# Two-layer graph kernel: the maxima of gathered neighbours accumulate in a PSUM bank, the third and fourth tile come earlier in the program, and layer 0 and the neighbour codes share one bank

## The reference, cut to what matters

```
h = relu(layernorm(x))                                   # (8, 2048, 256)
idx = the 25 smallest j with adj[n, j] != 0              # per node
agg = max over idx of h[idx]          (>= 0 if there are 25 or fewer)
x = x + relu(concat(h, agg) @ W0 + b0)                   # layer 0
h = relu(layernorm(x));  hidden = h @ W1.T
attn = leaky_relu(hidden @ a[0] + (hidden @ a[1]).T), masked, softmax
x = x + attn @ hidden + bias                             # layer 1
```

## Time and profile before

| what | value |
|---|---|
| median of 3 runs | 4676.5 us (4674.2 to 4679.66) |
| the profiled execution, its own time | 4680.8 us |
| its span, first to last instruction | 4679.0 us |
| GpSimd busy | 3481.4 us (74%) in 3204 instructions |
| VectorE busy | 2768.3 us (59%) |
| TensorE matmul busy | 2578.4 us (55%), mean granted clock 0.714 of full speed |
| ScalarE busy | 1470.9 us (31%) |

### The profile page before, as it was taken

How to read it: one execution, slowest core, us unless ns; L and a number is a source line. 1 busy time by engine, 2 the same in 40 slices (tenths; PEclk the granted TensorE clock), 3 DMA queues, 4 the chain that set the end, 5 groups by cost and what they waited for, 6 DMA issues and landing times.

```text
span 4679.0 us, 39010 instructions
## 1 busy us (share of the span) xinstructions
PE 2578.4 (55%) x10074; PEld 1682.2 (36%) x10074; DVE 2768.3 (59%) x6213; ACT 1470.9 (31%) x1489; POOL 3481.4 (74%) x3204
## 2 busy tenths in 40 slices
PE   1222245565655565655566565565665556565589
PEld 0111133343433343333344333343443334343356
DVE  5444456566666565665665665656666556665655
ACT  3111233323333232333232333332333323333234
POOL 5777777777777777777777777777777777777730
PEclk7555566777766777776677767677776777776789
DMA  7444555545555545555555555554555554544430
GB/s 265 159 149 156 171 174 177 193 160 189 185 178 195 173 165 194 174 180 199 169 182 179 177 177 197 171 193 162 181 182 188 184 182 159 186 169 153 147 109 32
DMA packets 228389, 809.23 MB, mean 173 GB/s; under 512 B 59466, under 2 KB 60372, under 8 KB 207828
## 3 DMA queue, kind: packets, MB, share of 16 engines
q0 software_dynamic: 153600, 419.64, 28.9%
q1 hardware_dynamic: 56308, 321.91, 18.7%
q10 hardware_dynamic: 18432, 67.12, 3.5%
HBM read 690.98 MB, written 119.54 MB: 173 GB/s over the span
## 4 chain that ended last, share of the span: by engine, by line
POOL 74%; issue 21%; PE 3%; DMA 1%; ACT 0%; DVE 0%; POOLq 0%; SPq 0%; DVEq 0%; ACTq 0%
POOL near L461 74%; PE acc L1302 2%; PE pen L1291 0%; PE pen L1288 0%; DMA nmask_dram<-nm_t 0%; DMA adj_i<-in_adj_dram 0%; DMA table_dram<-near 0%; DVE near L836 0%; ACT near L665 0%; PE bank L1273 0%; PE acc L1263 0%; ACT nm_t L506 0%; POOLq L458 0%; PE bank L1241 0%; DMA near<-table_dram,idx 0%
## 5 line engine op out<-in xcount | busy, mean ns | idle before, releaser
L461 POOL DMA_INDIRECT near<-table_dram,idx x3200 | 3481.2, 1088 | 1012.9 <-issue 975.2
L836 DVE TENSOR_TENSOR near<-near 128x3072 f32<-128x3072 f32 (+3 forms) x512 | 866.0, 1691 | 1214.6 <-DMA near<-table_dram,idx 1200.8
L1302 PE MATMUL acc<-hid,wgt 128*128 (+1 forms) x4096 | 1012.0, 405 | 79.2 <-ACT wgt L544 76.2
L1302 PEld LDWEIGHTS acc<-hid,wgt 128*128 128x128 f32 x4096 | 812.9, 203 | 206.4 <-issue 79.7
L1233 PE MATMUL bank<-cst,h_q 128*128 128x128 f32 x256 | 84.5, 431 | 1304.0 <-DVE agg L839 1292.7
L614 ACT ACTIVATE h_t<-bank 128x512 f32<-128x512 f32 x128 | 76.4, 597 | 1739.9 <-PE bank L1235 1739.9
L1241 PE MATMUL bank<-w_sb,h_t 128*128 128x256 f32 x1024 | 476.7, 646 | 98.0 <-ACT h_t L614 98.0
L1233 PEld LDWEIGHTS bank<-cst,h_q 128*128 128x128 f32 x256 | 35.5, 195 | 1346.5 <-DVE agg L839 1102.0
L506 ACT ACTIVATE nm_t<-adj_i,big_c 128x2048 bf16<-128x2048 int32 x128 | 499.8, 3954 | 5.0 <-DMA adj_i<-in_adj_dram 5.0
L924 DVE SCALAR_TENSOR_TENSOR wgt<-pen,a_slope,lin 128x512 f32<-128x512 f32 x512 | 361.1, 746 | 223.3 <-PE pen L1291 172.3
L539 ACT ACTIVATE lin<-a_b,a_rise 128x512 f32<-128x512 f32 x468 | 317.3, 718 | 430.8 <-DVE wgt L924 408.2
(11 more groups left out here) (137 smaller groups left out, 2125.5 us busy)
## 6 DMA issues: line engine op xcount, KB each, us to landing
adj_i<-in_adj_dram SPq DMA_DIRECT2D x128, 1024.0 KB
nmask_dram<-nm_t ACTq DMA_DIRECT2D x128, 512.0 KB, 7.6
nm_q<-nmask_dram SPq DMA_DIRECT2D x29, 2048.0 KB, 8.4
near<-table_dram,idx POOLq DMA_INDIRECT x3200
h_q<-table_dram SPq DMA_DIRECT2D x32, 512.0 KB, 3.9
x_q<-in_x_dram SPq DMA_DIRECT2D x32, 512.0 KB, 5.0
xmid_dram<-x_q SPq DMA_DIRECT2D x32, 512.0 KB
o_q<-xmid_dram SPq DMA_DIRECT2D x32, 512.0 KB, 6.3
```

The lines of the kernel that those rows point to most:

```text
L461: pool.indirect_dma_start(out=near[:, t % 2, k, :], out_offset=None, in_=table, in_offset=bass.IndirectOffsetOnAxis(ap=idx[:, t, k:k + 1], ...
L836: nc.vector.tensor_tensor(rows[:, lo:count, :], rows[:, lo:count, :], rows[:, other:other + count, :], ALU.max).then_inc(mx_step, 1)
L1302: mm = nc.tensor.matmul(acc[:, t, 0:C + 1], wgt[:, c % 2, i * QR + t * P:i * QR + (t + 1) * P], hid[:, bass.ds(batch * NJ + j, 1), 0:C + 1 ...
```

## The change

The maxima no longer fold `near` onto itself. The first `tensor_tensor` of a tile takes two pairs of rows (512 elements each) from `near` and writes `highest`, a PSUM tile of one bank; ten more take the next pair from `near` and `highest` and write `highest` again; then row 25 with the first half of `highest` goes to `agg`, and `agg` with its second half to `agg`. `agg` now has two halves in turn. `highest` takes the place of `bank2`, so the neighbour codes and layer 0's output go through `bank1` as well, and each user of `bank1` on TensorE waits for both semaphores that free it (`bank_free`). In VectorE's order the maxima of tile 2 move into the index rounds of pair 0 (`third_tile`), those of tile 3 ahead of chunk 4; TensorE and ScalarE do `layer0` 2 and 3 and their copies after chunks 1 and 4 in place of 3 and 7; `index_prep` of pair 0 comes after `attend_setup` on TensorE.

```diff
-        agg = sb("agg", [P, C], F32)
+        agg = sb("agg", [P, 2, C], F32)
-        bank2 = psum("bank2", [P, 512], F32)
+        highest = psum("highest", [P, 2 * C], F32)
@@ ScalarE, step @@
-                for c in range(1, 4):
+                for c in range(1, 8):
                     attended(c)
-                gathered()
-                for c in range(4, 8):
-                    attended(c)
-                gathered()
+                    if c in (1, 4):
+                        gathered()
@@ VectorE, index_words and residual0 read bank1 in place of bank2 @@
-                words = bank2[:, :].rearrange("p (u g) -> p u g", u=2)
+                words = bank1[:, :].rearrange("p (u g) -> p u g", u=2)
@@ VectorE, maximum @@
-                rows = near[:, t % 2, :, :]
-                folds = [(0, 12, 13), (0, 6, 7), (0, 3, 4), (0, 2, 2)]
-                for n, (lo, count, other) in enumerate(folds):
-                    nc.vector.tensor_tensor(rows[:, lo:count, :], rows[:, lo:count, :],
-                                            rows[:, other:other + count, :], ALU.max).then_inc(mx_step, 1)
-                    dve.wait_ge(mx_step, n + 1)
-                nc.vector.tensor_tensor(agg[:, :], rows[:, 0, :], rows[:, 1, :], ALU.max).then_inc(agg_made, 1)
+                pair = lambda k: near[:, t % 2, k:k + 2, :].rearrange("p a c -> p (a c)")
+                mx_n = Count()
+                nc.vector.tensor_tensor(highest[:, :], pair(0), pair(2), ALU.max).then_inc(mx_step, 1)
+                for k in range(4, S - 1, 2):
+                    dve.wait_ge(mx_step, mx_n.next())
+                    nc.vector.tensor_tensor(highest[:, :], pair(k), highest[:, :], ALU.max).then_inc(mx_step, 1)
+                dve.wait_ge(mx_step, mx_n.next())
+                nc.vector.tensor_tensor(agg[:, t % 2, :], near[:, t % 2, S - 1, :], highest[:, 0:C], ALU.max
+                                        ).then_inc(mx_step, 1)
+                dve.wait_ge(mx_step, mx_n.next())
+                nc.vector.tensor_tensor(agg[:, t % 2, :], agg[:, t % 2, :], highest[:, C:2 * C], ALU.max).then_inc(agg_made, 1)
@@ VectorE, step @@
-                def after_first():
+                def third_tile():
                     finished(1)
+                    gathered(2)
                     attended(2)
 
+                def fourth_tile():
+                    finished(3)
+                    attended(6)
+
                 if "index" in stages:
-                    index_write(0, woven(after_first, 1, 3))
+                    index_write(0, woven(third_tile, 1, 3))
+                    finished(2)
                     index_words(s + 1, 1)
...
-                gathered(2)
+                gathered(3)
                 attended(4)
-                finished(2)
-                rest = "index" in stages and lo < LAST - 1
-                if rest:
-                    ix_n = woven(lambda: attended(6), 5, 7)
+                if "index" in stages and lo < LAST - 1:
+                    index_write(1, woven(fourth_tile, 5, 7))
                 else:
-                    attended(5, 6, 7)
-                gathered(3)
-                if rest:
-                    index_write(1, ix_n)
+                    attended(5)
+                    fourth_tile()
+                    attended(7)
                 if "attend" in stages:
                     attend_end(a)
-                finished(3)
@@ TensorE @@
+            def bank_free():
+                pe.wait_ge(b1_free, b1.n + 1)
+                pe.wait_ge(b2_free, b2.n + 1)
...
                 gathered(0)
+                if "attend" in stages:
+                    attend_setup(a)
                 if "index" in stages:
                     index_prep(s + 1, 0)
-                if "attend" in stages:
-                    attend_setup(a)
                 gathered(1)
-                for c in range(4):
+                for c in range(8):
                     if "attend" in stages:
                         chunk(a, c)
+                    if c == 1:
+                        gathered(2)
                     if "index" in stages and c == 2:
                         index_prep(s + 1, 1)
-                gathered(2)
-                for c in range(4, 8):
-                    if "attend" in stages:
-                        chunk(a, c)
-                gathered(3)
+                    if c == 4:
+                        gathered(3)
```

More of the change, by code:

```diff
@@ L1254, in project @@
                 pe.wait_ge(h2t_made, q + 1)
-                pe.wait_ge(b1_free, b1.next())
+                bank_free()
+                b1.next()
                 for k in range(KC):
```

29 lines of the change are left out of this document (17 added, 12 removed).

## The result

| | before | after |
|---|---|---|
| median of 4 runs each, us | 4677.1 (4674.2 to 4679.7) | 4282.5 (4277.5 to 4284.6) |
| after over before | | 0.9151, interval 0.9139 to 0.9162 |
| the profiled execution, its own time / its span | 4680.8 / 4679.0 | 4277.5 / 4275.7 |

The kernel is 8.5% faster. The forecast was 4276.5 us (4250 to 4375).

The account below looks back on a forecast made before the run. It took GpSimd's queue of 3200 gathers to bound the kernel: 4679.0 - 423 + 12 + 9 + 2 = 4279 span, 4281 its own time, 4276.5 us after allowing 4.3 to the median; range 4250 to 4375.

Parts of the forecast that it names:

- Which instructions stop a gather: GpSimd gathers: VectorE instructions with two SBUF inputs stop them while they last; those with one PSUM input do not.
- 423 us of folds: Gather time over the median owed to the in-place folds, which the change frees: 423 us, bounds 403 and 444.
- 12 us left at the first instruction: First maxima instruction of each tile still reads two SBUF tensors: 12 us of stretch stays, between none and 24.
- 0.69 us for a maximum with PSUM on both sides: Maxima on VectorE: each 512-element instruction that reads and writes PSUM priced at 0.69 us, like line 793.
- The bound from above of 1.4: Maxima on VectorE: 1.4 us per instruction if a PSUM write cost a full second pass; rival 4820 us, chance 0.04.
- VectorE's cycle 4 us under GpSimd's: VectorE's chain through a step: 121.2 us against 125.4 for 100 gathers, 4.2 under, so GpSimd stays the bound.
- The other two margins, 9 us each: Within a step: about 9 us to spare before GpSimd needs `agg`, and 9 before it needs pair 0's indices.
- The stop of 9 us in the last quad: Last quad: late maxima 0 delay pair 1's indices, so GpSimd stops once for 9 us (0 to 15).
- Gathers busy 3070, last gather at 4080, VectorE waiting under 500, +2 at the end: Signs of being right, in us, on the gather line and VectorE's waits; +2 is longer maxima after the last landing.
- the first case's own range: Whole kernel with GpSimd still the bound at 1.25 us a gather: 4243 to 4308 us, chance 0.74.
- the chain as a bound: Rival: VectorE's chain through a step becomes the bound, 4335 to 4520 us, most likely about 4370; chance 0.19.

Follow-up runs that it names:

- experiment 2: Changed kernel with its thirteen short maxima instructions accumulating in the first two rows of `near` in SBUF, not in PSUM: 4395.6 us, ratio 0.9407 to the kernel before.
- experiment 1: Changed kernel with the four in-place SBUF folds of before, new order and single bank kept: 4673.9 us, ratio 1.0011 to the kernel before.
- (4): Changed kernel with the first two-SBUF maximum replaced by a copy to PSUM and an eleventh maximum with PSUM: 4256.1 us, ratio 0.9109 to the kernel before.
- experiment 5: Changed kernel with maxima 0 and pair 1's indices ahead of the attention work in the last quad only: 4278.4 us, ratio 0.9158 to the kernel before.

## Why the prediction was right, step by step

The span fell by 403.3 us where the sum had 400. The gathers are busy 414.1 us less, GpSimd's idle time ahead of them grew by 10.1, and the tail by 0.8. That the forecast lies 6 us under the median is within what the runs of one kernel differ by.

- **Which instructions stop a gather.** Right. Two SBUF inputs do (experiment 2 in short ones, 1 in long ones), one input in PSUM doesn't, nor does a copy from SBUF to PSUM (4). The row on which the prediction rested for the PSUM side shows less than it was taken for: the gather of 2337.00 wants its turn 0.17 us after the start of line 793, where two SBUF inputs might not have held it either. But of the 12 gathers in that trace that meet line 793 over 0.18 us after its start none takes over 0.950. The Trainium skill (SBUF — State Buffer, Who interferes with whom) says that `tensor_tensor` was not seen to stall DMA; that is not so for these gathers, as 430 us of stretch stand at it in experiment 1. Its sentence that a VectorE instruction with two SBUF inputs contends with GpSimd instructions that read SBUF is borne out by the same 430 us, and the gathers' indices stand in SBUF. Its sentence on instructions with at most one SBUF input, which the prediction also used, holds outside the two-port performance modes, a condition that the prediction left out.
- **423 us of folds.** Measured in experiment 1 as 430, and 422 in the trace of before, within the bounds of 403 and 444. The prediction gave the change the whole of it; experiment 2 shows that two thirds would have come from shorter instructions alone, which it did not separate.
- **12 us left at the first instruction.** 13.2 us in 50 gathers. The number is right by luck. The prediction had any phase for half of the tiles, with a stretch wherever the 0.69 us lie across the gather's turn. By the narrower condition of experiment 2 only 0.52 us of them count, and any phase for all tiles gives 128 x 0.52 / 1.25 = 53 gathers of 0.26 us, 14 us (an estimate).
- **0.69 us for a maximum with PSUM on both sides.** 0.695 in 1280 of them. The bound from above of 1.4 was far off.
- **VectorE's cycle 4 us under GpSimd's.** The sign is right and the size low. In the step shown VectorE waits 0.23 + 9.00 us for gathers ahead of maxima 2 and 3, and 5.1 to 9.3 in steps 12 to 27. I took the pieces of the sum with the waits they had before; which of them shrank I did not trace. The other two margins, 9 us each, were right: 10.4 to 11.7 for `agg` (9.2 in the steps before), 6.8 to 11.5 for the indices of pair 0.
- **The stop of 9 us in the last quad.** The place and the reason are right, and 11.1 us were measured. That it costs its length is not borne out: taken away in experiment 5, at the price of later attention work, it gives nothing, and the rows of 2.16 and 4.93 us put its own cost at no more than about 7 (an estimate). It was a term of the sum that should have been weighed against what bounds the end.
- **Gathers busy 3070, last gather at 4080, VectorE waiting under 500, +2 at the end.** 3067, 4089.6, 439, and +0.8 us. By the prediction's own terms the last gather should have been put at 4493.7 - 423 + 12 + 9 = 4091.7; the 4080 was a slip in the working and not in the sum. The upper end of the first case's own range, 4308, is one too: with 403, 24 and 15 it is 4314, and the lower end, 4243, keeps the stop at 9.
- **What it missed.** It priced the new order and never the old one, which is 0.4% or 18 us better on these chips. And it gave 0.19 to the chain as a bound, with a lower clock and hidden handoffs as what could lengthen it; on two chips late copies and gaps between instructions do, and the sign of the result turns.

## What to carry to other kernels

A gather from GpSimd that takes longer than its fellows is to be laid beside VectorE's timeline: if an instruction that reads two SBUF tensors ends a constant time before it, give that instruction a PSUM operand, or at least make it short, since the gather waits for one instruction and not for the row of them. Before an order is changed to make room, measure the room that the old one leaves; and a stop near the end is only worth removing if what follows it would be ready sooner. A margin of a few per cent on the second-longest engine can be gone on another chip, so a change that lengthens that engine's work is to be timed on more than one.

## What was not expected of the hardware

- An instruction on two SBUF tensors holds only the gathers that want their turn later than about 0.17 us after its start: over 0.18 us all 1135 of experiments 1 and 2 are stretched, within 0.165 none of 178.
- Between two instructions on two SBUF tensors that are 0.03 us apart a waiting gather gets in: 635 gathers beside line 836 in experiment 2 lose 0.205 us each, not the 7 us of the row.
- VectorE writes a PSUM bank as fast as SBUF: 695 ns for 512 float32 against 693 in experiment 2, and a copy of 512 float32 from SBUF to PSUM takes 695 and stretches no gather.
- On two chips the kernel before takes 24% longer and the kernel after 43% (6106 against 0.9151 x 4673). In the one trace of the latter VectorE's and ScalarE's busy times and the median gather are within 0.5% of the old ones. The time goes into one copy of ScalarE a step that starts 38 to 48 us after its input is ready (line 614, 1245 us in all) and into gaps of 0.7 us and more between instructions; the profile names nothing that ends the longest of them but "issue" and "remote".
